# Another order of the same tasks on four engines in a software-pipelined attention loop

## Chip, cores and metric

One core of one Trainium2 chip runs the whole program. The metric is the device time of one execution in microseconds (us), the median of the runs shown.

## What is computed

A transformer layer with adaptive layer norms on 8 samples of 512 tokens with 256 features: a gated delta-rule attention (16 key heads, 32 value heads, head size 128) and a small mixture of experts. Nearly all the time goes to the attention. Cut to what matters:

```python
qkvz = hidden_states @ W_qkvz.T                  # q, k, v, z of all heads
mixed = silu(causal_conv4(q, k, v))              # 4 taps along the tokens
q, k = l2norm(q), l2norm(k)
g = cumsum(-exp(A_log) * softplus(a + dt_bias))  # inside a chunk
decay = where(tril, exp(g_i - g_j), 0)
A = -where(strict_tril, (k * beta) @ k.T * decay, 0)
T = solve_triangular(eye - A, eye)               # the inverse, chunk by chunk
value_, k_cumdecay = T @ v_beta, T @ (k_beta * exp(g))
for each chunk:                                  # scan with a state of 128 x 128
    v_new = v_i - kcd_i @ state
    out_i = (q_i * exp(g_i)) @ state + (q_i @ k_i.T * decay) @ v_new
    state = state * exp(g_last) + (k_i * exp(g_last - g_i)).T @ v_new
h = out * rsqrt(mean(out**2) + eps); h = norm_weight * h * silu(z)
y = h @ W_out.T
```

## The kernel before

Three stages run one after the other: `modulation_and_gates`, `attention` and `experts`. The change touches the attention stage alone.

**The loop.** The attention stage has 128 steps, one for each sample b and key head kh (8 x 16). A step handles one key head with its two value heads, in four chunks of 128 tokens, that is eight 128 x 128 units (U = 8). Its work is cut into tasks: 57 on PE, 63 on DVE, 41 on ACT, 16 on POOL. Each engine walks through its own list of tasks over and over: `PE_ORDER`, `ACT_ORDER`, `DVE_ORDER`, `POOL_ORDER` (lines 34 to 44). `M2@3` in the list means: part 2 of task M, for the step that lies 3 ahead of the number of this round. So one round of a list holds tasks of several steps, and a step goes through the engines over some four rounds. `loop` (in `attention`) writes the rounds before the first and after the last out in full and runs the middle ones two at a time in a hardware loop; how many are written out follows from `LEAD`, the largest number behind an @ in any list.

**What sets the order.** Within an engine, the list alone. Between engines, semaphores: each task waits for the tasks whose results it reads and for those that still read what it overwrites (`t.wait`), whatever the lists say. Nothing is planned at run time. SP, which issues the loads, has an order of its own (`FEEDS`), which no list touches.

**The tasks that matter here,** with the lines that the profile shows:

- P0 to P11 (PE, L658): the projections, two matmuls to a bank; C (ACT, L886) and T0 to T11 (DVE, L1018) do the convolution.
- KT, QT (PE, L668, L676): transposes of keys and queries; KN, QN on ACT square them, KN, QN on DVE (L1024, L1028) sum the squares. PW (POOL, L1199) takes the root of the sums.
- SM0 to SM3 (DVE, L1034, L1038, L1043, L1046): tiny operations of 128 x 8 elements that turn the roots into the factors `neg_c`. SM2 reads `inv` and `g_col`, SM3 `cc` and `inv`. SN0 (L1052) reads `neg_c` and `g_col` and makes `w_c`; SN1 (L1056) and SN2 (L1060) make scales of q. All these tensors lie in SBUF.
- KK0, KK1 (PE, L690): the products of keys with keys and queries into the two banks `p_out`. GL (POOL, L1194) and GE (ACT, L924, eight `Exp` and a load of the activation table) make `dec`, of which there is one buffer. GA0 to GA3 (DVE, L1072, eight operations) multiply the products with `neg_c` and `dec` into `ga`.
- SL (POOL, L1203), AB0 and AB1 (DVE, L1078), AO (ACT, L929), AR and AL (POOL, L1209, L1213) prepare the matrix A. L, M1 to M5 and Y1 to Y5 (PE), q1 to q5, y0 to y5, X1 to X5 (DVE, L1085, L1093, L1102), and XB1 to XB5 on ACT (L936) and on POOL (L1225) invert it level by level in one bank `p_lev`. s10, s11 (L1109), XD, Q6, p6, Z6, YC, XC join the halves.
- D0, D1 (PE, L764 to L766) compute the residual, F0, F1 (DVE, L1118) write it to `resid`, RL (POOL, L1217) splits it, G0, G1 (PE, L780), v0, v1 (ACT, L970), W0, W1 (PE, L796 to L798), IV0, IV1 (ACT, L966) finish the inverse.
- TR, VW, U, ST, KS, RR, SD, VX, O, OT, VK: the scan over the four chunks, on all engines. OQ, OS, OP, ON, HT: the norm of the output. OY0, OY1 (PE, L868): its projection, into the banks `p_out`; YA0, YA1 (DVE, L1170) add it up.

KT, VT, QT, KK, D, G, W, ON and OY share the two banks `p_out`. Each of them waits for the reader of what stood in the bank last (`wait_newest`, whose argument lists the other users of the bank, newest first). GL waits for GE of the step before, and GE for two things, in this order:

```python
elif name == "GE":
    t.wait(act, "g_low")
    t.wait(act, "ga_done", back=1)
    for u in range(U):
        last = act.activation(dec[:, u, :], low[:, u, :], ACT.Exp, bias=g_neg[p][:, u:u + 1])
    last.then_inc(s["decay"], 1)
```

Of the kernel before, what the change touches and what calls it, by code (L numbers as in the profile page):

```python
# [16 lines left out]
KT = D // P  # L17
# [13 lines left out]
Q_G, Q_BETA, Q_W, Q_EG, Q_GL = range(5)  # L31
NQ = 5
PAD = TAPS - 1
PE_ORDER = ("M2@3 ON1@1 O0@2 VT0@3 Y2@3 KS1@2 W1@2 M3@3 TR1@2 P0@4 Y3@3 U1@2 P1@4 M4@3 KS2@2 O1@2 P2@4 Y4@3 TR2@2 "
            "P3@4 M5@3 VT1@3 O2@2 U2@2 P4@4 KS3@2 Y5@3 P5@4 KT@4 QT@4 XD@3 Q6@3 TR3@2 P6@4 Z6@3 P7@4 D0@3 O3@2 XC@3 "
            "D1@3 KK0@4 KK1@4 P8@4 OY0@1 OY1@1 G0@3 L@4 P9@4 W0@3 M1@4 P10@4 TR0@3 Y1@4 G1@3 P11@4 U0@3 ON0@2")
ACT_ORDER = ("GE@2 OT3@0 C3@2 OQ3@0 XC@1 SV0@2 AO@2 v0@1 IV0@1 XB1@2 VX0@1 v1@1 SV1@2 XB2@2 OT0@1 Z0@2 Z1@2 XB3@2 "
             "IV1@1 VK0@2 VX1@1 C0@3 XB4@2 OT1@1 OQ0@1 VX2@1 C1@3 OQ1@1 XB5@2 OT2@1 VK1@2 OQ2@1 SK@3 SQ@3 C2@3 KN@3 "
             "QN@3 XD@2 VX3@1 KT@3 YC@2")
DVE_ORDER = ("T10@3 y0@3 T11@3 X1@3 q1@3 YA1@0 VW0@2 y1@3 X2@3 ST0@2 HT0@1 q2@3 HT1@1 y2@3 RR1@2 X3@3 q3@3 VW1@2 "  # L40
# [3 lines left out]
POOL_ORDER = ("SL@3 OP@1 XB1@3 ON@1 XB2@3 SD1@2 GL@4 XB3@3 QD@3 XB4@3 AR@3 SD2@2 AL@3 XB5@3 PW@4 RL@3")  # L44


def const_columns():
# [347 lines left out]
def attention(nc, io, scratch, const):  # L395


    with ExitStack() as ctx:
# [66 lines left out]
        SPARE = 3  # L465
        LEAD = max(int(name[-1]) for order in (PE_ORDER, ACT_ORDER, DVE_ORDER, POOL_ORDER) for name in order.split())

# [42 lines left out]
        def loop(eng, emit, order):  # L510
            for iteration in range(-LEAD, 0):
                run(eng, emit, order, fixed(iteration))
            rounds = (NIT - LEAD) // 2
            with eng.Fori(0, rounds) as m:
                for u in range(2):
                    run(eng, emit, order, lambda off: Step(m * 2 + (u + off), (u + off) % 2, m + (u + off) // 2))
            for iteration in range(rounds * 2, NIT):
                run(eng, emit, order, fixed(iteration))
# [126 lines left out]
        def _(pe):  # L645
# [225 lines left out]

            loop(pe, emit, PE_ORDER)

        @block.scalar
        def _(act):
# [120 lines left out]

            loop(act, emit, ACT_ORDER)

        @block.vector
        def _(dve):  # L1000
# [171 lines left out]

            loop(dve, emit, DVE_ORDER)

        @block.gpsimd
        def _(pool):
# [77 lines left out]

            loop(pool, emit, POOL_ORDER)

# [390 lines left out]
```

## Time and profile before

| | |
|---|---|
| median of 3 runs | 4839.93 us (4837.36 to 4840.07) |
| span of the profiled execution | 4831.3 us |
| PE, PE weight loads | busy 97%, 66% |
| DVE, ACT, POOL | busy 91%, 72%, 57% |
| DMA | 24.7% of 16 engines, 78 GB/s |
| mean granted TensorE clock | 0.987 |

The profile is of one execution. Busy time of an engine is the union of its instructions; overlapping ones count once. Line numbers (L658) are those of the kernel before. In a timeline, a record gives start, duration and what was executed, and in brackets the idle time of the engine ahead of it, if it is long, with the instruction that ended it. Neighbours of the same line are put together (x8), and their durations are then the stretch from the first start to the last end. The clock is a fraction of 2.4 GHz.

### The profile page before, as it was taken

How to read it: one execution, taken by the hardware profiler on the slowest of the kernel's cores; microseconds unless marked ns; L12 is line 12 of the kernel's file. 1: busy time of each engine (PE TensorE's matmuls, PEld its weight loads, DVE VectorE, ACT ScalarE, POOL GpSimd, SP SyncE). 2: the span in 40 equal slices, each digit the busy share in tenths (PEclk: the TensorE clock that was granted, in tenths of full speed). 3: DMA queues.
4: the chain of work that ended last, by engine and by line, in shares of the span. 5: the costliest groups of instructions: out<-in, count | busy, mean ns of one | idle time of the engine just before them, and what ended most of it. 6: DMA issues, size and time to landing. Idle time of an engine off the chain costs nothing. (4 is left out here: it accounts for less than half of the span.)

```text
span 4831.3 us, 132942 instructions
## 1 busy us (share of the span) xinstructions
PE 4671.0 (97%) x38533; PEld 3195.1 (66%) x38788; DVE 4411.5 (91%) x9152; ACT 3467.6 (72%) x8336; POOL 2743.0 (57%) x2329
## 2 busy tenths in 40 slices
PE   5899999999999999999999999999999999999978
PEld 3566666666666666666666666666666666666643
DVE  4899999999999999999999999999999999999953
ACT  3677777777777777777777777777777777777732
POOL 2456665656565665656566665656566665656520
PEclk7999999999999999999999999999999999999988
DMA  4222222222222222222222222222222222222122
GB/s 156 65 75 79 68 86 70 88 66 87 67 79 79 68 86 71 88 66 87 67 80 79 68 86 66 92 66 84 70 78 80 66 87 66 92 66 84 55 79 83
DMA packets 185165, 377.26 MB, mean 78 GB/s; under 512 B 86400, under 2 KB 95744, under 8 KB 184960
## 3 DMA queue, kind: packets, MB, share of 16 engines
q1 hardware_dynamic: 185088, 376.46, 24.7%
q14 instruction: 57, 0.47, 0.0%
q8 instruction: 20, 0.33, 0.0%
HBM read 360.13 MB, written 16.25 MB: 78 GB/s over the span
## 5 line engine op out<-in xcount | busy, mean ns | idle before, releaser
L658 PE MATMUL p_proj<-hid,w_in 128*128 128x512 f32 x3072 | 1626.7, 612 | 30.0 <-POOL ident_h L1185 28.9
L1018 DVE SCALAR_TENSOR_TENSOR conv<-p_proj,taps,conv 128x509 f32<-128x509 f32 (+2 forms) x1536 | 1134.8, 739 | 48.2 <-ACT conv L886 34.9
L1199 POOL TENSOR_TENSOR root<-sums,half_pow 128x8 f32<-128x8 f32 x128 | 210.8, 1647 | 862.9 <-DVE sums L1028 843.9
L1225 POOL TENSOR_SCALAR_AFFINE_SELECT x_bd<-x_t 128x512 bf16<-128x512 bf16 x640 | 422.6, 660 | 213.5 <-DVE x_t L1102 211.2
L658 PEld LDWEIGHTS p_proj<-hid,w_in 128*128 128x128 f32 x3072 | 497.3, 192 | 55.1 <-POOL ident_h L1185 29.1
L1093 DVE TENSOR_TENSOR y_h<-p_lev,y_h 128x512 bf16<-128x512 f32 x640 | 440.2, 688 | 74.4 <-PE p_lev L725 74.4
L868 PE MATMUL p_out<-h_t,w_out 128*128 128x512 f32 x1024 | 476.5, 608 | 2.2 <-DVE h_t L1164 1.1
L936 ACT ACTIVATE x_bd<-x_t 64x512 bf16<-64x512 bf16 x640 | 397.7, 621 | 96.3 <-DVE x_t L1102 96.2
L1102 DVE STREAM_TRANSPOSE x_t<-y_h 128x512 bf16<-128x512 bf16 x640 | 450.3, 704 | 4.5
L1072 DVE SCALAR_TENSOR_TENSOR ga<-p_out,neg_c,dec 128x256 f32<-128x256 f32 x1024 | 412.9, 477 | 35.4 <-ACT dec L924 34.8
L886 ACT ACTIVATE conv<-p_proj,taps 128x512 f32<-128x512 f32 x512 | 351.7, 687 | 121.9 <-PE p_proj L658 119.3
L1085 DVE TENSOR_TENSOR q_h<-p_lev,consts 128x512 bf16<-128x512 f32 x640 | 429.6, 671 | 3.8 <-PE p_lev L718 3.8
L979 ACT ACTIVATE vx<-p_b 128x256 f32<-128x256 f32 x512 | 197.9, 386 | 285.8 <-PE p_b L816 161.4
L1217 POOL TENSOR_TENSOR r_lo<-resid 128x1024 bf16<-128x1024 f32 x128 | 242.3, 1893 | 247.9 <-DVE resid L1118 247.9
L838 PE MATMUL p_b<-vx,ga 128*128 128x128 f32 x2048 | 375.1, 275 | 0.0
L868 PEld LDWEIGHTS p_out<-h_t,w_out 128*128 128x128 f32 x1024 | 184.6, 190 | 285.0 <-DVE ga L1072 147.9
L725 PEld LDWEIGHTS p_lev<-q_h,x_bd 128*128 128x128 bf16 x5120 | 216.5, 97 | 213.5 <-issue 101.5
L985 ACT ACTIVATE o_tok<-p_b 128x256 f32<-128x256 f32 x512 | 194.1, 379 | 199.5 <-PE p_b L838 196.4
L718 PEld LDWEIGHTS p_lev<-y_h,a_bd 128*128 128x128 bf16 x5120 | 222.7, 98 | 152.1 <-issue 84.2
L1232 POOL TENSOR_TENSOR q_dec<-kq,e_row 128x512 f32<-128x512 f32 x256 | 320.0, 1271 | 0.0
L924 ACT ACTIVATE dec<-low,g_neg 128x128 f32<-128x128 f32 x1024 | 313.3, 388 | 1.6
L1244 POOL TENSOR_TENSOR o_sc<-o_sc,neg_half 128x8 f32<-128x8 f32 x128 | 211.4, 1651 | 168.9 <-DVE o_sc L1159 168.9
(213 smaller groups left out, 12562.4 us busy)
## 6 DMA issues: line engine op xcount, KB each, us to landing
w_in<-in_w_in SPq DMA_DIRECT2D x128, 768.0 KB, 6.3
g_row<-rows_scratch SPq DMA_DIRECT2D x128, 512.0 KB, 3.2
hid<-h_scratch SPq DMA_DIRECT2D x128, 512.0 KB, 7.4
e_row<-exp_rows_scratch SPq DMA_DIRECT2D x128, 512.0 KB, 5.3
w_out<-in_w_out SPq DMA_DIRECT2D x128, 256.5 KB, 2.7
x<-in_x SPq DMA_DIRECT2D x8, 512.0 KB, 10.6
h_scratch<-x SPq DMA_DIRECT2D x8, 512.0 KB, 2.6
y_scratch<-y_acc SPq DMA_DIRECT2D x8, 512.0 KB, 6.1
```

The costliest lines, as they stand in the source:

```text
L658: last = pe.matmul(p_proj[tile % 2][:], w_in[p][:, kt, tile * P:(tile + 1) * P], hid[p][:, kt, :], start=(kt == 0), stop=(kt == KT - 1))
L838: last = pe.matmul(p_b[:, at], ga[p][:, n * HD + h, 1, :], vx[:, h, :], start=(n == 0), stop=True)
L868: last = pe.matmul(p_out[n][:], w_out[p][:, h * D + n * P:h * D + (n + 1) * P], h_t[:, :, h, :], start=(h == 0), stop=(h == HD - 1))
L886: act.activation(conv[:, n, :], p_proj[n % 2][:], ACT.Copy, scale=taps[p][:, n, PAD:PAD + 1])\
L936: act.activation(x_bd[0:HB, :, 0:HB], x_t[0:HB], ACT.Copy).then_inc(s["xbd"], 1)
L1018: dve.scalar_tensor_tensor(conv[:, tile, late:], p_proj[tile % 2][:, 0:S - late], taps[p][:, tile, j:j + 1], conv[:, tile, late:], ALU.mul ...
L1072: last = dve.scalar_tensor_tensor(ga[p][:, u], kk, neg_c[p][:, n, h:h + 1], each(dec[:, u, :], 2), ALU.mult, ALU.mult)
L1085: dve.tensor_tensor(q_h[:], levels(), each(const["mask"][:, n * HB:(n + 1) * HB], U), ALU.mult)\
L1093: dve.tensor_tensor(y_h[:], levels(), y_h[:], ALU.add).then_inc(s["y_done"], 1)
L1102: dve.transpose(x_t[:].rearrange("p u f -> p (u f)"), y_h[:].rearrange("p u f -> p (u f)"))\
L1225: pool.affine_select(x_bd[:, :, HB:P], x_t[:], [[0, U], [0, HB]], ALU.is_ge, zero, base=-HB, channel_multiplier=1).then_inc(s["xbd_low"], 1)
L1232: last = pool.tensor_tensor(q_dec[p][:, :, h, :], kq[p][:, :, 1, :], e_row[p][:].rearrange("p (c h) i -> p c h i", h=HD)[:, :, h, :], ALU. ...
```

## The change

The four lists are replaced by others. They hold the same tasks; in each list some stand in another place, and some are taken from another step. The order in which the tasks use the two banks `p_out` is the same as before in either bank, and the lists in `wait_newest` stay as they are. The largest number behind an @ becomes 5 (GL@5), so that one more round is written out ahead of the loop and the hardware loop ends earlier.

```diff
-PE_ORDER = ("M2@3 ON1@1 O0@2 VT0@3 Y2@3 KS1@2 W1@2 M3@3 TR1@2 P0@4 Y3@3 U1@2 P1@4 M4@3 KS2@2 O1@2 P2@4 Y4@3 TR2@2 "
-            "P3@4 M5@3 VT1@3 O2@2 U2@2 P4@4 KS3@2 Y5@3 P5@4 KT@4 QT@4 XD@3 Q6@3 TR3@2 P6@4 Z6@3 P7@4 D0@3 O3@2 XC@3 "
-            "D1@3 KK0@4 KK1@4 P8@4 OY0@1 OY1@1 G0@3 L@4 P9@4 W0@3 M1@4 P10@4 TR0@3 Y1@4 G1@3 P11@4 U0@3 ON0@2")
-ACT_ORDER = ("GE@2 OT3@0 C3@2 OQ3@0 XC@1 SV0@2 AO@2 v0@1 IV0@1 XB1@2 VX0@1 v1@1 SV1@2 XB2@2 OT0@1 Z0@2 Z1@2 XB3@2 "
-             "IV1@1 VK0@2 VX1@1 C0@3 XB4@2 OT1@1 OQ0@1 VX2@1 C1@3 OQ1@1 XB5@2 OT2@1 VK1@2 OQ2@1 SK@3 SQ@3 C2@3 KN@3 "
-             "QN@3 XD@2 VX3@1 KT@3 YC@2")
-DVE_ORDER = ("T10@3 y0@3 T11@3 X1@3 q1@3 YA1@0 VW0@2 y1@3 X2@3 ST0@2 HT0@1 q2@3 HT1@1 y2@3 RR1@2 X3@3 q3@3 VW1@2 "
-             "y3@3 ST1@2 X4@3 q4@3 T0@4 RR2@2 T1@4 y4@3 VW2@2 X5@3 T2@4 q5@3 T3@4 ST2@2 T4@4 T5@4 y5@3 SN1@3 s11@3 "
-             "s10@3 RR3@2 T6@4 p6@3 KN@4 QN@4 T7@4 T8@4 SN2@3 F0@3 SM0@4 SM1@4 SM2@4 SM3@4 F1@3 SN0@3 GA0@4 GA1@4 "
-             "GA2@4 GA3@4 T9@4 YA0@1 OS0@2 AB0@4 AB1@4 OS1@2")
-POOL_ORDER = ("SL@3 OP@1 XB1@3 ON@1 XB2@3 SD1@2 GL@4 XB3@3 QD@3 XB4@3 AR@3 SD2@2 AL@3 XB5@3 PW@4 RL@3")
+PE_ORDER = ("ON0@1 O0@2 ON1@1 KS1@2 Y2@3 VT0@3 W1@2 M3@3 TR1@2 P0@4 Y3@3 U1@2 P1@4 M4@3 KS2@2 O1@2 Y4@3 P2@4 TR2@2 P3@4 U2@2 "
+            "VT1@3 O2@2 KS3@2 M5@3 P4@4 KT@4 Y5@3 P5@4 QT@4 Q6@3 XD@3 P6@4 TR3@2 Z6@3 P7@4 D0@3 D1@3 O3@2 KK0@4 XC@3 KK1@4 "
+            "P8@4 OY0@1 OY1@1 G0@3 L@4 P9@4 W0@3 M1@4 P10@4 TR0@3 G1@3 Y1@4 P11@4 U0@3 M2@4")
+ACT_ORDER = ("XD@1 QN@2 YC@1 OQ0@0 VX3@0 OQ1@0 SV0@2 OT3@0 OQ2@0 XC@1 OQ3@0 C3@2 GE@3 v0@1 IV0@1 XB1@2 v1@1 VX0@1 SV1@2 XB2@2 "
+             "Z0@2 OT0@1 XB3@2 Z1@2 AO@2 VX1@1 VK0@2 C0@3 XB4@2 IV1@1 OT1@1 VX2@1 C1@3 VK1@2 XB5@2 SK@3 OT2@1 SQ@3 KN@3 KT@3 "
+             "C2@3")
+DVE_ORDER = ("YA1@0 q1@3 VW0@2 y1@3 X2@3 ST0@2 q2@3 HT0@1 HT1@1 y2@3 RR1@2 X3@3 q3@3 VW1@2 SN1@3 y3@3 ST1@2 X4@3 q4@3 T0@4 "
+             "RR2@2 T1@4 y4@3 VW2@2 X5@3 T2@4 ST2@2 T3@4 T4@4 q5@3 T5@4 SN2@3 y5@3 s11@3 s10@3 RR3@2 p6@3 T6@4 T7@4 KN@4 QN@4 "
+             "T8@4 F0@3 F1@3 SM0@4 SM1@4 SM2@4 SN0@3 SM3@4 GA0@4 GA1@4 GA2@4 GA3@4 T9@4 YA0@1 OS0@2 AB0@4 AB1@4 T10@4 OS1@2 "
+             "y0@4 T11@4 X1@4")
+POOL_ORDER = ("OP@1 XB1@3 ON@1 XB2@3 XB3@3 SD1@2 XB4@3 QD@3 SD2@2 XB5@3 AR@3 AL@3 PW@4 RL@3 GL@5 SL@4")
```

Read round the circle, and with the steps counted from the same task, the lists differ in these places:

- PE: M2 ahead of ON0; O0 between ON0 and ON1; KS1 ahead of Y2 and VT0 behind it; Y4 ahead of P2; U2 ahead of VT1 and O2; KS3 ahead of M5 and P4; KT ahead of Y5; Q6 ahead of XD; P6 ahead of TR3; D1 right behind D0, XC between KK0 and KK1; G1 ahead of Y1.
- DVE: ST2 ahead of T3; q5 between T4 and T5; SN2 ahead of y5, SN1 behind VW1; p6 ahead of T6, T7 ahead of the two sums; F1 right behind F0; SN0 between SM2 and SM3; OS1 behind T10; YA1 ahead of q1; q2 ahead of HT0.
- ACT: GE from right behind YC to right behind C3, for the next step; OQ0 to OQ2 and OT2 later, by up to half a round; QN behind XD; SV0 ahead of OT3; v1 ahead of VX0; OT0 between Z0 and Z1's new place behind XB3; AO from ahead of v0 to behind Z1; IV1, VK1 and KT in other places by one to four tasks.
- POOL: GL from behind SD1 to right behind RL, ahead of SL; SD1 behind XB3; QD behind XB4, AR and AL behind XB5.

## Rows read from the trace of the kernel before

**Rows 1.** The page, one line of its 40 slices: granted TensorE clock in tenths.
```profile
PEclk7999999999999999999999999999999999999988
```
**Rows 2.** One line's instructions: count, ns min/median/max, first and last start in us.
```profile
L1072 DVE SCALAR_TENSOR_TENSOR ga<-p_out,neg_c,dec x1024: 473/476/485, 134.2 to 4592.7; 128x256 f32<-128x256 f32 x171
```
**Rows 3.** Timeline of DVE, 2410.9 to 2418.8 us: start, duration, engine, line, operation.
```profile
2410.89 0.68 DVE L1028 TENSOR_REDUCE sums<-squares 128x4 f32<-128x512 f32 x1
...
2413.05 0.16 DVE L1060 TENSOR_SCALAR q_s<-inv 128x4 f32<-128x4 f32 x1
2413.12 0.69 DVE L1118 TENSOR_TENSOR resid<-p_out,consts 128x512 f32<-128x512 f32 x1
2413.72 0.17 DVE L1034 TENSOR_SCALAR neg_n<-root 128x8 f32<-128x8 f32 x1
...
2414.36 0.17 DVE L1046 SCALAR_TENSOR_TENSOR neg_c<-cc,inv 128x8 f32<-128x8 f32 x1
2414.47 0.69 DVE L1118 TENSOR_TENSOR resid<-p_out,consts 128x512 f32<-128x512 f32 x1
...
2415.57 3.23 DVE L1072 SCALAR_TENSOR_TENSOR ga<-p_out,neg_c,dec 128x256 f32<-128x256 f32 x8 [0.33 <-ACT dec L924]
```
**Rows 4.** Timeline of POOL, from 2402 to 2429 us, same columns.
```profile
2402.55 1.89 POOL L1213 TENSOR_TENSOR a_lo<-a_rest 128x1024 bf16<-128x1024 f32 x1
2404.40 0.66 POOL L1225 TENSOR_SCALAR_AFFINE_SELECT x_bd<-x_t 128x512 bf16<-128x512 bf16 x1
...
2411.80 1.65 POOL L1199 TENSOR_TENSOR root<-sums,half_pow 128x8 f32<-128x8 f32 x1 [6.74 <-DVE sums L1028]
2415.24 1.89 POOL L1217 TENSOR_TENSOR r_lo<-resid 128x1024 bf16<-128x1024 f32 x1 [1.79 <-DVE resid L1118]
...
2428.41 2.35 POOL L1194 TENSOR_TENSOR low<-g_row,consts 128x1024 f32<-128x1024 f32 x1
```
**Rows 5.** Timelines of DVE and POOL, around 207 us and around 4624 us.
```profile
207.40 0.71 DVE L1156 TENSOR_TENSOR o_sc<-o_ss,q_s 128x8 f32<-128x8 f32 x1
207.00 1.10 POOL L1203 TENSOR_SCALAR_AFFINE_SELECT ga<-ga 128x1024 f32<-128x1024 f32 x1 [1.81 <-DVE ga L1072]
...
4624.25 0.26 DVE L1156 TENSOR_TENSOR o_sc<-o_ss,q_s 128x8 f32<-128x8 f32 x1
4622.59 1.89 POOL L1217 TENSOR_TENSOR r_lo<-resid 128x1024 bf16<-128x1024 f32 x1 [8.39 <-DVE resid L1118]
```
**Rows 6.** Timeline of PE, 2407 to 2421 us.
```profile
2407.44 0.60 PE L668 MATMUL p_out<-consts,kq 128*128 128x128 f32 x4
...
2411.67 0.22 PE L764 MATMUL p_out<-y_dn,ga 128*128 128x128 bf16 x1
...
2416.24 1.02 PE L658 MATMUL p_proj<-hid,w_in 128*128 128x512 f32 x2
2417.28 3.70 PE L868 MATMUL p_out<-h_t,w_out 128*128 128x512 f32 x8
```
**Rows 7.** Timeline of ACT, 2411 to 2422 us, and one row of 4738.87 us.
```profile
2411.62 1.28 ACT L924 ACT_TABLE_LOAD   x1
2412.92 2.45 ACT L924 ACTIVATE dec<-low,g_neg 128x128 f32<-128x128 f32 x8
...
2421.24 0.60 ACT L970 ACTIVATE g_t<-p_out 128x512 bf16<-128x512 f32 x1 [0.52 <-PE p_out L780]
...
4738.87 1.28 ACT L1466 ACT_TABLE_LOAD   x1 [12.08 <-PE p_h L1397]
```
**Rows 8.** Timeline of PE, the filling of the loop: 172 us and 209 us.
```profile
172.25 0.61 PE L713 MATMUL p_lev<-eye_h,a_bd 128*128 128x64 bf16 x8 [3.27 <-DVE a_bd L1078]
...
209.05 0.61 PE L713 MATMUL p_lev<-eye_h,a_bd 128*128 128x64 bf16 x8 [3.12 <-DVE a_bd L1078]
```
**Rows 9.** Busy us (and instructions) by window; then granted clock, DMA share, GB/s.
```profile
171.39:178.22 6.83, 5.75 (x32) 3.74 (x34) 4.09 (x7) 2.14 (x4) 0.66 (x1) 0.50 0.29 90
...
208.94:212.35 3.41, 3.08 (x16) 1.81 (x18) 2.75 (x6) 0.29 (x1) 2.29 (x3) 0.50 0.38 147
```

## Prediction

> **Names.** Tasks are named without their @; times behind "F0 at 0" are in us from F0's start. F is the pair of `resid` adds on DVE, SM0 to SM3 and SN0 the tiny 128x8 operations behind the key norms, GA the eight gated products, PW, RL, GL, SL the POOL tasks of L1199, L1217, L1194, L1203, GE the eight exponentials of L924, OY the output projection, L the first matmul group of a solve, KK the products of keys.
>
> **What bounds the kernel now.** First the page: its slices show PE at 9 tenths in all the middle, with TensorE's granted clock at 1.00 there, the 2.4 GHz level, and lower only at both ends [rows 1]. Then the period. The eight GA of a step are 128 groups between 134.2 and 4592.7 us; the last start is the eighth of its group, some 2.75 us behind the first, so a step takes (4592.7 - 2.75 - 134.2) / 127 = 35.08 us [rows 2]. The loop is 127 periods of the 4831; everything else here is a sum within one period. Then the timelines of the engines. PE has hardly a hole, and DVE neither: in the stretch from the key sums to GA, only GA waits, 0.33 us, for GE [rows 3]. So no engine has a large reserve. What the order can lose is much larger than what it can win: a new wait on DVE that PE cannot pass lengthens every period by itself.
>
> **The order around the key norms.** Before, from F0 on DVE: F0 at 2413.12, SM0 at 2413.72 (0.60 later), SM3 at 1.24 with SM1 and SM2 in between, F1 at 1.35, then SN0, GA at 2.45 [rows 3]. On POOL, PW runs from 2411.80 to 2413.45, and then nothing until RL at 2415.24, which is 0.08 behind the end of F1 (2414.47 + 0.69) [rows 4]. So SM2, SM3 and SN0, which read two tensors of SBUF each, all fall into a time in which POOL is idle.
>
> The new lists put F1 right behind F0, ahead of SM0, and SN0 between SM2 and SM3; POOL gets GL right behind RL. RL waits for F1 alone, since PW ends earlier. With F0 at 0: F1 ends at 0.60 + 0.69 = 1.29, RL starts at 1.37 and ends at 3.26. SM0 needs PW: the second key sum started at 2410.89, SM0 at 2413.72, 2.83 later and nearly all of it PW [rows 3, 4]. Between that sum and F0 stands now only T8, at 0.71 + 0.66, so SM0 can't start before 2.83 - 1.37 = 1.46, which is inside RL. SM3 stood 0.64 behind SM0 [rows 3], SM2 0.2 ahead of SM3, so SM2 comes to about 1.90.
>
> **What a two-input operation does under POOL.** The trace has it twice, where OS0, the same 128x8 shape as SM2 and SM3 (SM3 0.17 us [rows 3]), runs while POOL reads SBUF. In the filling of the loop it starts at 207.40 under SL (207.00 to 208.10) and takes 0.71 us; in the draining it starts at 4624.25 under RL (4622.59 to 4624.48) and takes 0.26. Both end within 0.03 us of the end of POOL's operation [rows 5]. So SM2 is held until 3.27. SM3 needs SM2's result and starts 0.03 later, at 3.30. But POOL starts a queued task before the last one's record ends: a_lo at 2402.55 takes 1.89, and the next started at 2404.40 [rows 4]. GL, whose waits are long met, starts at 1.37 + 1.85 = 3.22, ahead of SM3, and takes 2.35 [rows 4]: to 5.57. SM3 ends there, and GA0 starts at 5.65; 5.9 if SN0 is the one held and SM3 follows it. Before it was 2.45. **This is +3.2 us on DVE** (3.45 at the upper end; 0.8 at the lower, if GL lets SM3 pass). The 0.33 us that GA waited for GE is won back inside this number.
>
> The Trainium skill, SBUF — State Buffer, section Who interferes with whom, says the same of two SBUF inputs, and adds that `tensor_scalar` and copies in a 2-port mode are held too. The row of SN2, a `tensor_scalar`, speaks against the addition for this shape: it took 0.16 us at 2413.05, under PW [rows 3, 4]. SN2 moves to just ahead of y5, where the last POOL task is AL; by that rule y5 would be held for up to 0.8 us more per period, some 100 us in all. I leave it out of the sum.
>
> **Who waits for GA.** OY0 overwrites the bank that GA0 and GA1 read, and PE is in order. PE's part from D0 to the end of P8 is the same work as before: it started at 2411.67, 1.45 ahead of F0, and ended at 2416.24 + 1.02, so at F0 + 4.1 [rows 6]. OY0 can start when GA1 ends; GA0 and GA1 are half of 3.23 [rows 3]: 5.65 + 1.65 + 0.05 = 7.35. Before, it started at 2417.28 with P8 just in front [rows 6]. So PE stands still for 3.2 us in each period.
>
> **The rest of the period.** From GA to the next F0 it was 35.08 - 2.45 = 32.6 us. SL still waits for GA (it started right behind it, and GL has ended by then), so AB and L keep their distance. GE's new place is behind C3 and ahead of v0: it can start when GA ends, 5.65 + 3.23 = 8.9, its table load (1.28) having run under GA, and with 2.45 it ends at 11.35 [rows 7]; v0 needs G0, behind the 3.70 of OY, about 7.35 + 3.7 + 0.2 = 11.25 [rows 6]. It costs nothing there, as long as GA is late. The second load goes from SV0 to SV1, between VX0 and XB2; XB2 then ends some 0.1 us ahead of the time at which PE comes to Y2. The transposes KT, 0.60 us by their record [rows 6], of which the next group overlaps a part, now stand ahead of Y5, so y5 is 0.4 later. On the other side q2 ahead of HT0, KS1 ahead of Y2, YA1 ahead of q1 and Y4 ahead of P2 take waits of a tenth or two away, each below what a row names as idle; my estimate from the starts is 0.8 in all, between 0.4 and 1.2. AO, OQ0 to OQ2, AR, AL, SD1 and M5 move inside slack of more than a microsecond. Net -0.4, between -0.8 and 0. The period is 5.65 + 32.2 = 37.85 us, at full clock.
>
> **The clock.** Twice in the filling PE stood still for about as long as it now will in each period: 3.27 us before 172.25, 3.12 before 209.05 [rows 8]. After both the granted clock was 0.50, the 1.2 GHz level, for 6.83 and 3.41 us, with PE busy 5.75 and 3.08 us of it [rows 9]. Work at half clock loses half of its time: 2.9 and 1.5 us, 2.2 on average. OY, G0, L and P9 stand there, and after GA's delay PE is the last to arrive. I count three of four gaps: +1.7, bounds 0 and 2.9. Period 39.5.
>
> **Sum.** (39.5 - 35.1) x 126 = 4.4 x 126 = 555, on the profiled span of 4831: 5386. The median of the runs, 4839.9, lies 8.6 us above that span: **5395 us**. Filling and draining have the same tasks (one more unrolled step at each end, which only holds GL); I count nothing. No DMA gets on the path: g_row is fetched a period before GL.
>
> **Rivals.** (1) The lock as above, but the clock stays at 2.4 GHz after most gaps: 37.85, + 2.8 x 126 = 350, so 5190 us. For it: two gaps are few, they lie in the filling, where other waits surround them, and the loop's gap has unbroken work on both sides. Against it: the gaps are as long as these [rows 8, 9]. (2) DVE gets its turn between RL and GL, or SBUF reads don't collide in steady state. Then GL becomes the bound in another way. GE needs GL's end, and its table load stands behind that wait: at 4738.87 a load came only after 12.08 us of idle [rows 7], behind the first wait of its instruction. From F0: 1.29 to F1's end, then 0.08 + 1.85 + 2.35 + 0.1 + 1.28 + 2.45 = 8.1 to v0. From v0 to the next F0 it was 2413.12 + 35.08 - 2421.24 = 27.0 [rows 3, 7], less the 0.4 from above: 36.0, or 35.6 if v0's slack of some 0.4 before W0 is used up. That gives + 0.55 to 0.9 x 126: 4910 to 4955. The skill, ScalarE: Activation LUTs, section What ACT_TABLE_LOAD costs, adds a drain of about 1.38 us to a load; in the rows the exponentials start 0.02 us behind the load's end [rows 7], so I give it nothing. (3) **Faster**: no collision, and the load runs ahead of GL's wait. Then GE costs nothing, the short waits are won, F0 to GA takes 2.3 in place of 2.45, and PE has nearly no wait left: 35.08 - 0.4 - 0.15 = 34.5 us, -0.58 x 126 = -73, so 4767. It needs SM3 to end by 2.3 behind F0, and v0 to start within 0.3 us of G0's end; it decides at SM2's duration, 0.17 or over a microsecond. Against it stand both rows of OS0. (4) No change: (2) with errors of sum that cancel.
>
> **Chances.** Forecast 0.57, (1) 0.25, (2) 0.11, (3) 0.04, (4) 0.03. The range of the first two is 5130 (rival 1 with the rest at -0.8) to 5620 (every gap at half clock, GA at 5.9), 8 in 10 with their tails. About 0.2%, 10 us, is what can be told from no change: faster 0.04, same 0.03, slower 0.93.
>
> **What would show it.** Right: SM2 at 1.4 us and SM3 or SN0 at over 2 in place of 0.17; GA idle before it for a few tenths at most, since the time is in the durations; PE idle about 3.2 us before L868, released by GA of L1072; clock at 0.5 in many slices; GE's idle before L924 gone. Wrong: SM2 at 0.17 (the lock falls), PE gaps without a lower clock (the 1.7 falls), or idle before L970 put down to L924 (rival 2).

## The result and the profile after

The changed kernel takes **5456.02 us** (median of 4 runs, 5450.64 to 5458.91) against 4838.65 (4836.20 to 4840.07): the ratio is 1.1275, with a 95% interval of 1.1259 to 1.1291. The forecast was 5395 in a range of 5130 to 5620. The profiled execution has a span of 5455.8 us, 624.5 more than before, with the same work.

The page of the changed kernel: the granted clock, and three rows of its groups (busy us, mean ns of one, then idle time before them and what ended it).

```profile
PEclk7899999999999999999999999999999999999999
...
L868 PE MATMUL p_out<-h_t,w_out 128*128 128x512 f32 x1024 | 644.9, 789 | 429.6 <-DVE ga L1072 428.5
...
L924 ACT ACTIVATE dec<-low,g_neg 128x128 f32<-128x128 f32 x1024 | 313.0, 387 | 273.0 <-DVE ga L1072 245.9
...
L1072 DVE SCALAR_TENSOR_TENSOR ga<-p_out,neg_c,dec 128x256 f32<-128x256 f32 x1024 | 412.9, 476 | 14.4 <-DVE neg_c L1046 11.7
```

PE now stands still for 429.6 us ahead of OY, 3.4 in each step, and GA ends that. One matmul of OY takes 789 ns on average; it took 608. The lines of DVE (count, ns min/median/max, first and last start) say why GA is late:

```profile
L1072 DVE SCALAR_TENSOR_TENSOR ga<-p_out,neg_c,dec x1024: 473/476/485, 138.1 to 5219.2; 128x256 f32<-128x256 f32 x171
...
L1043 DVE TENSOR_TENSOR cc<-inv,g_col x128: 168/1512/1601, 137.7 to 5214.5; 128x8 f32<-128x8 f32 x128
...
L1046 DVE SCALAR_TENSOR_TENSOR neg_c<-cc,inv x128: 166/2273/2277, 137.9 to 5216.1; 128x8 f32<-128x8 f32 x128
...
L1052 DVE TENSOR_TENSOR w_c<-neg_c,g_col x128: 152/154/156, 172.5 to 5250.2; 128x8 f32<-128x8 f32 x128
...
L1060 DVE TENSOR_SCALAR q_s<-inv x128: 306/1142/1466, 162.6 to 5240.9; 128x4 f32<-128x4 f32 x128
```

The period is (5219.2 - 2.75 - 138.1) / 127 = 39.99 us, where it was 35.08 [rows 2]. SM2 and SM3 take 1.51 and 2.27 us in place of 0.17 [rows 3]; and SN2 takes 1.14 in place of 0.16. The timelines of DVE and then POOL (start, duration) show beside what they run:

```profile
2406.32 1.14 DVE L1060 TENSOR_SCALAR q_s<-inv 128x4 f32<-128x4 f32 x1
...
2413.26 1.28 DVE L1118 TENSOR_TENSOR resid<-p_out,consts 128x512 f32<-128x512 f32 x2
2414.58 0.17 DVE L1034 TENSOR_SCALAR neg_n<-root 128x8 f32<-128x8 f32 x1
2414.79 0.20 DVE L1038 RECIPROCAL inv<-neg_n 128x8 f32<-128x8 f32 x1
2415.03 1.51 DVE L1043 TENSOR_TENSOR cc<-inv,g_col 128x8 f32<-128x8 f32 x1
2416.46 0.15 DVE L1052 TENSOR_TENSOR w_c<-neg_c,g_col 128x8 f32<-128x8 f32 x1
2416.57 2.27 DVE L1046 SCALAR_TENSOR_TENSOR neg_c<-cc,inv 128x8 f32<-128x8 f32 x1
2418.88 3.23 DVE L1072 SCALAR_TENSOR_TENSOR ga<-p_out,neg_c,dec 128x256 f32<-128x256 f32 x8
```
```profile
2405.54 1.90 POOL L1213 TENSOR_TENSOR a_lo<-a_rest 128x1024 bf16<-128x1024 f32 x1
2412.91 1.64 POOL L1199 TENSOR_TENSOR root<-sums,half_pow 128x8 f32<-128x8 f32 x1 [5.47 <-DVE sums L1028]
2414.62 1.89 POOL L1217 TENSOR_TENSOR r_lo<-resid 128x1024 bf16<-128x1024 f32 x1
2416.47 2.35 POOL L1194 TENSOR_TENSOR low<-g_row,consts 128x1024 f32<-128x1024 f32 x1
```

SM2 ends with RL (2416.54 and 2416.51), SM3 with GL (2418.84 and 2418.82), SN2 with AL (2407.46 and 2407.44). Below, such an operation is said to be held by the POOL task beside it. GA starts 5.62 us behind F0. PE and ACT behind it:

```profile
2416.21 1.02 PE L658 MATMUL p_proj<-hid,w_in 128*128 128x512 f32 x2
2420.59 3.70 PE L868 MATMUL p_out<-h_t,w_out 128*128 128x512 f32 x8 [3.36 <-DVE ga L1072]
```
```profile
2418.92 1.28 ACT L924 ACT_TABLE_LOAD   x1 [1.71 <-POOL low L1194]
2422.14 2.45 ACT L924 ACTIVATE dec<-low,g_neg 128x128 f32<-128x128 f32 x8 [1.94 <-DVE ga L1072]
2424.56 0.60 ACT L970 ACTIVATE g_t<-p_out 128x512 bf16<-128x512 f32 x1
```

In this step OY ran at full clock, 3.70 us. In the next it took 5.40, and the view of a stretch in it shows the 1.2 GHz level, right behind a gap of 3.52 us (the columns are those of [rows 9]):

```profile
2459.42 5.40 PE L868 MATMUL p_out<-h_t,w_out 128*128 128x512 f32 x8 [3.52 <-DVE ga L1072]
```
```profile
2459.93:2463.34 3.41, 3.41 (x5) 1.35 (x4) 2.07 (x5) 2.37 (x8) 1.10 (x1) 0.50 0.00 0
```

From 400 to 5000 us, 115 periods, the trace has 82 such stretches, 65 of 3.41 us and 17 of 6.83. Of 110 middle steps the 31 whose OY ran at full clock take 38.75 us, all together 40.00.

### The profile page after: what moved, and what is told of

Same layout as the page of the kernel before. It is cut to its first block and busy times, and to the rows that moved or that the text cites. A ratio compares the mean times of both kernels' runs of the same rounds, so it can differ in the third digit from the quotient of the medians.

```text
span 5455.8 us, 133429 instructions
## 1 busy us (share of the span) xinstructions
PE 4839.6 (89%) x38788; PEld 3291.8 (60%) x38788; DVE 4949.2 (91%) x9152; ACT 3519.1 (65%) x8334; POOL 2759.7 (51%) x2329
## 5 line engine op out<-in xcount | busy, mean ns | idle before, releaser
L658 PE MATMUL p_proj<-hid,w_in 128*128 128x512 f32 x3072 | 1657.7, 622 | 32.3 <-POOL ident_h L1185 28.7
L868 PE MATMUL p_out<-h_t,w_out 128*128 128x512 f32 x1024 | 644.9, 789 | 429.6 <-DVE ga L1072 428.5
L868 PEld LDWEIGHTS p_out<-h_t,w_out 128*128 128x128 f32 x1024 | 243.7, 249 | 822.3 <-DVE ga L1072 554.4
L924 ACT ACTIVATE dec<-low,g_neg 128x128 f32<-128x128 f32 x1024 | 313.0, 387 | 273.0 <-DVE ga L1072 245.9
L1203 POOL TENSOR_SCALAR_AFFINE_SELECT ga<-ga 128x1024 f32<-128x1024 f32 x128 | 140.6, 1098 | 453.1 <-DVE ga L1072 453.1
L970 ACT ACTIVATE g_t<-p_out 128x512 bf16<-128x512 f32 x256 | 152.8, 597 | 267.0 <-PE p_out L780 266.2
L994 ACT ACTIVATE o_junk<-o_tok 128x128 f32<-128x128 f32 x1024 | 303.3, 299 | 3.2
```

Source lines behind the costliest of these rows:

```text
L658: last = pe.matmul(p_proj[tile % 2][:], w_in[p][:, kt, tile * P:(tile + 1) * P], hid[p][:, kt, :], start=(kt == 0), stop=(kt == KT - 1))
L868: last = pe.matmul(p_out[n][:], w_out[p][:, h * D + n * P:h * D + (n + 1) * P], h_t[:, :, h, :], start=(h == 0), stop=(h == HD - 1))
```

## The experiments

Periods are worked out from the first and last GA, as above. "F0 to GA" and "gap", PE's idle time ahead of OY, are means over 110 middle steps of the trace. "Stretches" counts those at a granted clock of 0.50 in the loop, per 100 periods. The ratio is to the kernel before on the same chip.

| kernel | us | ratio (95%) | period | F0 to GA | gap | stretches |
|---|---|---|---|---|---|---|
| before | 4838.65 | 1 | 35.08 | 2.47 | none | 0 |
| changed | 5456.02 | 1.1275 (1.1259 to 1.1291) | 39.99 | 5.70 | 3.4 | 71 |
| e2_one_input | 4987.52 | 1.0312 (1.0294 to 1.0329) | 36.25 | 2.44 | 0.2 | 0 |
| e4_gl_back | 5090.21 | 1.0522 (1.0504 to 1.0539) | 37.06 | 3.70 | 1.4 | 0 |
| e3_f1_back | 5181.41 | 1.0711 (1.0693 to 1.0729) | 37.78 | 2.85 | none | 0 |
| e1_fill_pe | 5310.20 | 1.0982 (1.0964 to 1.1001) | 38.78 | 5.70 | 0.9 | 0 |
| e6_sn2_back | 5507.54 | 1.1392 (1.1373 to 1.1411) | 40.35 | 5.70 | 3.4 | 100 |
| e10_sn2_fill | 5220.39 | 1.0799 (1.0782 to 1.0816) | 38.08 | 5.71 | 0.9 | 0 |
| e7_before_f1 | 5146.63 | 1.0651 (1.0633 to 1.0669) | 37.54 | 4.44 | 2.1 | 30 |
| e11_before_f1_d1 | 4996.68 | 1.0335 (1.0320 to 1.0351) | 36.39 | 3.76 | 1.6 | 0 |
| e5_both_back | 4995.36 | 1.0338 (1.0320 to 1.0355) | 36.33 | 2.86 | none | 0 |
| e8_three_back | 4896.44 | 1.0133 (1.0116 to 1.0150) | 35.56 | 2.79 | none | 0 |
| e9_t7_back | 4818.66 | 0.9969 (0.9957 to 0.9981) | 34.95 | 2.25 | none | 0 |

**The inputs alone.** The order stays, the operations read one SBUF tensor each:

```diff
-  dve.tensor_scalar(neg_n[p][:], root[:], 1e-6, -1.0, ALU.add, ALU.mult)
+  dve.tensor_scalar(neg_n[p][:], root[:], 1e-6, -16.0, ALU.add, ALU.mult)
-  dve.tensor_tensor(cc[:], inv_k, beta, ALU.mult)
+  dve.reciprocal(cc[:], inv_k)
-  dve.scalar_tensor_tensor(neg_c[p][:], cc[:], -1.0, inv_k, ALU.mult, ALU.mult)
+  dve.reciprocal(neg_c[p][:], cc[:])
-  dve.tensor_tensor(w_c[p][:], neg_c[p][:], w, ALU.mult)
+  dve.reciprocal(w_c[p][:], over(neg_n[p][:, 0, :], [P, NC, HD]))
```

> The changed kernel with all lists and waits as they are, but SM2, SM3 and SN0 are reciprocals, which read one SBUF tensor in place of two (and the factor in SM0 is -16 in place of -1, to keep numbers small). The factors beta and w are left out, so the result is another one; number, order, shapes and waits of the instructions stay. THEORY (the two SBUF inputs are held by POOL): each takes about 0.2 us, GA starts at F0 + 2.6 in place of 5.7. Then GL sets the end: RL and GL end at F0 + 5.6, the table load at 6.95, GE at 9.4, v0 there, and from v0 to the next F0 27.35 us as in the changed kernel at full clock: 36.75 us per period, 4839 + (36.75 - 35.07) x 126 = 5050 us (4990 to 5110), clock at 1.00 in nearly all steps. RIVAL A (the long durations are a wait for RL's or GL's result or of DVE's pipeline, whatever the inputs): 5456, the three operations at 1.46 and 2.27. RIVAL B (no bound behind the hold): GE is no limit, 35.8 us per period, 4930.

```profile
L1043 DVE RECIPROCAL cc<-inv x128: 202/203/206, 137.4 to 4741.7; 128x8 f32<-128x8 f32 x128
...
L1046 DVE RECIPROCAL neg_c<-cc x128: 202/203/204, 137.6 to 4741.9; 128x8 f32<-128x8 f32 x128
```

Both take 0.20 us in all steps, although they run wholly beside RL, so it is neither the order nor a wait. The factors beta and w are left out here, and the operation changed together with what it reads. That it isn't the kind of operation, GA shows: it is a `SCALAR_TENSOR_TENSOR` as SM3 is, but takes one large input from a PSUM bank, and its eight run in 3.23 us partly beside RL [rows 3, 4], none longer than 0.485 us [rows 2]. In e3_f1_back they stand beside RL (2446.37 to 2448.27) and GL, and over 370 of them ran wholly under each, in at most 0.48 us:

```profile
2446.28 3.22 DVE L1072 SCALAR_TENSOR_TENSOR ga<-p_out,neg_c,dec 128x256 f32<-128x256 f32 x8
```

GL starts where it did, but SM3 is done by then. GA came 3.26 us earlier, and 3.74 us of period went, 1.24 of it the clock's part (below, with PE's gap filled). What is left is the rival with no collision (2), here in its timeline of ACT:

```profile
2352.45 1.28 ACT L924 ACT_TABLE_LOAD   x1 [1.73 <-POOL low L1194]
2353.74 2.45 ACT L924 ACTIVATE dec<-low,g_neg 128x128 f32<-128x128 f32 x8
2356.10 0.58 ACT L970 ACTIVATE g_t<-p_out 128x512 bf16<-128x512 f32 x1
```

GL, load, exponentials and v0 stand in a row. v0 starts at F0 + 9.31 (expected 9.4); from there to the next F0 it is 26.95 us, not 27.35, which together makes the run 62 us faster than expected, a little below its range.

**GL alone back:**

```diff
-  SD1@2 XB4@3 QD@3 SD2@2 XB5@3 AR@3 AL@3 PW@4 RL@3 GL@5 SL@4
+  SD1@2 GL@5 XB4@3 QD@3 SD2@2 XB5@3 AR@3 AL@3 PW@4 RL@3 SL@4
```

> The changed kernel with GL alone back behind SD1 on POOL; F1 stays ahead of SM0. THEORY: RL still holds SM2 for 1.4 to 1.5 us, but nothing follows RL, so SN0 and SM3 take 0.15 to 0.17 us. GA at F0 + 3.6 in place of 5.7, PE's gap ahead of OY 1.2 us and the clock at 1.00 behind it; GE starts when GA ends, at 6.85, v0 at 9.3, 9.3 + 27.35 = 36.65 us per period, 4839 + 1.58 x 126 = 5040 us (4990 to 5110). RIVAL (GL is not what holds SM3): SM3 stays at 2.27 us and the time near 5456.

```profile
L1043 DVE TENSOR_TENSOR cc<-inv,g_col x128: 166/1503/1599, 139.0 to 4844.5; 128x8 f32<-128x8 f32 x128
...
L1046 DVE SCALAR_TENSOR_TENSOR neg_c<-cc,inv x128: 166/167/169, 139.2 to 4846.1; 128x8 f32<-128x8 f32 x128
```

RL alone holds SM2, and SM3's hold goes with GL. GA is at F0 + 3.70 (3.6 expected). The time is 50 us above the expected one, because v0 comes at 9.41 and from there to the next F0 it takes 27.63 us.

**F1 and SN0 alone back:**

```diff
-  T8@4 F0@3 F1@3 SM0@4 SM1@4 SM2@4 SN0@3 SM3@4 GA0@4
+  T8@4 F0@3 SM0@4 SM1@4 SM2@4 SM3@4 F1@3 SN0@3 GA0@4
```

> The changed kernel with F1 and SN0 back where they were: F0, SM0 to SM3, F1, SN0, GA. All else stays, GL right behind RL too. THEORY: nothing two-input falls under POOL, SM2 and SM3 at 0.17 us, GA at F0 + 2.9 in place of 5.7. But RL now starts later, behind F1 at F0 + 2.8, so GL ends at 7.0, the table load at 8.4, GE at 10.85, v0 there: 10.85 + 27.35 = 38.2 us per period, 4839 + 3.1 x 126 = 5230 us (5150 to 5330, the upper part if the wait of W0 for v0 brings a low clock). So most of the loss stays although the hold is gone: a new wait in its place, ACT's v0 waiting for POOL's GL by way of the table load. RIVAL (the hold was all of it): GA at 2.9 gives a period of 35.9 at full clock, 4945 us.

Timelines of POOL and ACT of that run:

```profile
2446.37 1.90 POOL L1217 TENSOR_TENSOR r_lo<-resid 128x1024 bf16<-128x1024 f32 x1 [1.56 <-DVE resid L1118]
2448.22 2.36 POOL L1194 TENSOR_TENSOR low<-g_row,consts 128x1024 f32<-128x1024 f32 x1
```
```profile
2450.68 1.28 ACT L924 ACT_TABLE_LOAD   x1 [3.20 <-POOL low L1194]
2451.97 2.45 ACT L924 ACTIVATE dec<-low,g_neg 128x128 f32<-128x128 f32 x8
2454.32 0.57 ACT L970 ACTIVATE g_t<-p_out 128x512 bf16<-128x512 f32 x1
```

The hold ahead of GA is gone (SM2 and SM3 at 0.17 us), OY follows P8 without a gap, and still 2.7 us per period stay. The row that tells it is the load, which waits 3.20 us for GL. Under the hold the same chain was hidden: in the changed kernel the load ran under GA, and v0 started within 0.1 us of the end of G0. The later SL brings a new hold: OS0 (L1156, two SBUF inputs) takes 0.67 to 0.84 us to SL's end in every middle step, where it took 0.16. From v0 to the next F0 it is 26.95 us as in e2_one_input, where OS0 isn't held, so it shows no cost here.

**PE's gap filled:** three more products like P8's first, into the bank that P8 then overwrites.

```diff
+  for i in range(3 if n == 8 else 0):
+      pe.matmul(p_proj[0][:], w_in[p][:, 0, tile * P:(tile + 1) * P], hid[p][:, 0, :], start=True, stop=True)
```

> The changed kernel with the first product of P8 computed three more times into the same bank, so that PE has some 2.6 us of its own work inside the 3.4 us in which it waited for GA. Nothing that is used changes. THEORY (lock plus clock): in the changed kernel's trace 79 of 110 middle steps run OY wholly or partly at the 1.2 GHz level and take 40.49 us, the 31 others 38.75. With the gap cut to about 0.8 us the clock stays at 1.00, OY takes 3.70 us in every step, SM2 and SM3 stay at 1.46 and 2.27 us, the period is 38.75 and the time 5456 - (40.00 - 38.75) x 126 = 5298 us (5270 to 5330). RIVAL (the clock falls for another reason than the gap, or its fall costs nothing because DVE sets the period): 5456 or a little more, OY at 3.08 + 2.73 us on average as before.

```profile
2428.05 3.70 PE L869 MATMUL p_out<-h_t,w_out 128*128 128x512 f32 x8 [0.80 <-DVE ga L1073]
```
```profile
1000.00:2000.00 1000.00, 967.75 (x7871) 660.61 (x7869) 970.05 (x1803) 692.61 (x1655) 552.89 (x467) 1.00 0.22 70
```

PE has more to do, and the kernel is 146 us faster. The hold is the same (2.28 us on SM3), the clock is at 1.00, and the period is that of the full-clock steps. So the clock's part is 40.00 - 38.76 = 1.24 us per period.

**SN2 alone back:**

```diff
-  T5@4 SN2@3 y5@3 ... T8@4 F0@3
+  T5@4 y5@3 ... T8@4 SN2@3 F0@3
```

> The changed kernel with SN2 alone back behind T8, ahead of F0. In the changed kernel SN2 (a tensor_scalar of 128x4) starts under AL and takes 1.14 us in every step, ending with AL; before it took 0.16 under PW. THEORY (POOL holds the tensor_scalar too, and y5 to F0 is on the path): SN2 takes 0.16 us, the period loses 0.8 to 1.0 us of the 40.0, the clock's part stays: 5456 - 0.9 x 126 = 5345 us (5320 to 5390). RIVAL A (SN2 is late for another reason and takes as long in its new place, or SM0 comes later by as much): 5456. RIVAL B (DVE has slack there, the hold costs nothing): 0.16 us, but 5440 to 5460.

SN2 took 0.16 us as expected, and the kernel became 51 us slower: my expectation had the wrong sign. A window of it, in which OY took 6.58 us:

```profile
2438.95:2445.78 6.83, 5.84 (x7) 2.52 (x8) 5.11 (x13) 3.05 (x9) 1.10 (x1) 0.50 0.00 0
```

There are 114 stretches in 114 periods, 76 of them of 6.83 us, behind gaps no longer than in the changed kernel. To take the clock out, the next run has both edits:

> The changed kernel with SN2 back behind T8 and with the three extra products in PE's gap. SN2's move alone made the kernel slower (5508), although SN2 took 0.16 us in place of 1.14; OY was slowed in all of 110 middle steps in place of 79. THEORY (the move is worth 0.7 us per period, as with GL and F1 taken back, but more gaps end at the 1.2 GHz level): with the gap filled the clock stays at 1.00 and the period is 38.75 - 0.7 = 38.05, so 4834 + 2.98 x 126 = 5210 us (5180 to 5240), some 90 us below the filled kernel without the move (5310). RIVAL (the move itself costs time under the hold): at or above 5310.

38.08 against 38.78 us: without the clock, SN2's hold costs 0.70 us per period. With it, the gain was more than eaten up. Why nearly the same gap lowers the clock in 71 of 100 steps in one kernel and in all of the other stays open. In e6_sn2_back 94 of 113 neighbouring stretches start 40.96 us apart, and its steps take 39.5 to 41.1 us, so it looks as if it mattered where in time a gap falls; no run varied that alone.

**F1 alone, in the kernel before:**

```diff
-  F0@3 SM0@4 SM1@4 SM2@4 SM3@4 F1@3 SN0@3 GA0@4
+  F0@3 F1@3 SM0@4 SM1@4 SM2@4 SM3@4 SN0@3 GA0@4
```

> The kernel before with one move alone: F1 right behind F0, ahead of SM0. GL stays behind SD1, all other lists as before. THEORY: F1 ends at F0 + 1.29, RL starts at 1.37 and holds SM2 to 3.25, SM3 and SN0 follow at 0.17 each, GA at F0 + 3.6 in place of 2.47: + 1.1 us per period, PE's gap about 1.0 us with the clock at 1.00, 4837 + 1.1 x 126 = 4975 us (4940 to 5000). RIVAL (the hold comes only with the rest of the new order, or SM2 ends ahead of RL): SM2 at 0.17, within 10 us of 4837.

```profile
2420.82 0.69 DVE L1118 TENSOR_TENSOR resid<-p_out,consts 128x512 f32<-128x512 f32 x1 [0.59 <-PE p_out L766]
...
2421.86 1.65 DVE L1043 TENSOR_TENSOR cc<-inv,g_col 128x8 f32<-128x8 f32 x1
```
```profile
2421.59 1.90 POOL L1217 TENSOR_TENSOR r_lo<-resid 128x1024 bf16<-128x1024 f32 x1 [1.72 <-DVE resid L1118]
```

The hold was as expected; 172 us were missed by a wait. In the old PE order D1 stands behind O3 and XC, and F1, now early, waits for it. The gap became 2.1 us, and OY was slowed in 32 of 110 steps. With D1 right behind D0 as well:

```diff
-  D0@3 O3@2 XC@3 D1@3 KK0@4
+  D0@3 D1@3 O3@2 XC@3 KK0@4
```

> The kernel before with F1 right behind F0, as in the run that gave 5147, and with D1 on PE right behind D0, as in the changed kernel. In that run F1 waited 0.59 us for D1, RL started at F0 + 2.04 and GA came at F0 + 4.44, with PE's gap 2.09 us and OY at a lower clock in 32 of 110 steps. THEORY: without the wait RL starts at F0 + 1.36 and all of it comes 0.67 earlier: GA at F0 + 3.77, gap 1.4 us, the clock at 1.00 in all steps as behind the 1.45 us gap of the run with GL taken back, 36.4 us per period, 4834 + 1.33 x 126 = 5000 us (4970 to 5030). RIVAL (the wait for D1 was covered by the one for PW or by the hold): 5147.

GA at F0 + 3.76, 36.39 us, clock at 1.00: on the number. In the changed kernel, too, D1 stands behind D0; the two moves belong together.

**What is left of the loss.** Both moves back, with the edits of e3_f1_back and e4_gl_back together; then SN2 too, with that of e6_sn2_back; then T7 as well:

```diff
-  T6@4 T7@4 KN@4 QN@4 T8@4
+  T6@4 KN@4 QN@4 T7@4 T8@4
```

> The changed kernel with both moves taken back: F1 and SN0 behind SM3, GL behind SD1. Everything else of the change stays. THEORY: no two-input operation under POOL around the key norms and no GL ahead of GE. GA at F0 + 2.85, as measured with F1 alone taken back; the table load runs under GA, GE from 6.1 to 8.55, v0 at 8.6, then 26.95 us to the next F0, as in the two runs in which PE had no gap: 35.5 us per period, 4837 + 0.45 x 126 = 4893 us (4860 to 4940). So these two moves hold all but a percent of the loss. RIVAL (the rest of the new order costs much by itself): above 4940. RIVAL (the rest of the new order is a gain): below 4837.

> The changed kernel with three moves taken back: F1 and SN0, GL, and SN2 (behind T8). THEORY: as with the first two taken back (35.5 us per period), less the 0.5 to 1.0 us by which SN2's hold delays y5 and what follows it: 34.5 to 35.0 us, so 4770 to 4837, most likely 4820, and faster than the kernel before if the shorter waits of the new PE order are worth anything. RIVAL (PE or DVE work sets the period and SN2's hold was covered): the same as with two taken back.

> The kernel with three moves taken back, and with T7 too back behind the two key sums. With T7 ahead of them the sum of the queries stands only 1.4 us ahead of F0, PW ends 1.26 us behind F0, and DVE waits for it ahead of SM0; before, SM0 came 0.60 behind F0. THEORY: that wait is the rest of the loss against the kernel before (35.55 us per period against 35.07): SM0 at F0 + 0.60, GA at F0 + 2.2, the period 35.0 to 35.2, 4834 + 0.03 x 126 = 4838 us (4820 to 4855), no difference from the kernel before. RIVAL A (GE's new place or the new PE order holds the rest): 4880 to 4900 as without this move. RIVAL B (the new PE order is a gain once nothing hides it): below 4820.

The first came out 102 us above the expectation and the second 76, both outside their ranges. In both I had mis-stated v0 to the next F0. For the first I carried over 26.95 us from e2_one_input and e3_f1_back, in which v0 stood 1.2 and 2.3 us behind the end of G0; for the second I took SN2's hold off that figure once more. With v0 within 0.1 us of G0's end it is 27.60 with the hold and 26.91 without it, again 0.7. So behind a late v0 nearly all of SN2's hold was covered; this is argued from these figures, and no run tests it alone. What then still stood against the kernel before is a wait for PW, in the timelines of DVE with three moves back (first) and with T7 back (second):

```profile
2302.10 0.17 DVE L1034 TENSOR_SCALAR neg_n<-root 128x8 f32<-128x8 f32 x1 [0.57 <-POOL root L1199]
```
```profile
2264.25 0.16 DVE L1034 TENSOR_SCALAR neg_n<-root 128x8 f32<-128x8 f32 x1
```

Moving T7 is worth 0.61 us per period. The last kernel is **faster than both**: 4818.66 us, 0.31% below the kernel before (0.19 to 0.43). The expectation was 4838 (4820 to 4855), no difference. The kernel keeps the new PE and ACT lists, with GE in its new place; there the table load runs ahead of GA's end and GA no longer waits for GE. F0 to GA is 2.25 us in place of 2.47, and from GA to the next F0 nothing is won (32.68 us against 32.59). So the gain stands where GA waited for GE, not in the new PE order that rival B named; no run moved GE alone.

## Why the prediction was right, step by step

Over 110 middle steps a period grew by 4.93 us, from 35.07 to 40.00: 3.22 from F0 to GA, 0.70 for SN2, -0.23 for the rest of the order, and 1.24 for the clock. The forecast was 3.2, 0, -0.4 and 1.7. The hold, PE's gap and the clock were in their right places. That the sum came within 61 us is in part luck: the 0.70 that was left out is set off by 0.46 too much for the clock.

- **The hold.** SM0 at F0 + 1.32 (predicted 1.46), RL at 1.36 (1.37), GL at 3.21 (3.22), GA at 5.70 (5.65). Of the two ways in which SN0 and SM3 could follow RL the first holds: SN0 passes between RL and GL in 0.15 us in every step, SM3 is held to GL's end. That it is the second SBUF input, e2_one_input shows; that it is these two POOL tasks, e3_f1_back and e4_gl_back.
- **PE's gap.** 3.44 us on average for 3.2, released by GA, as said.
- **SN2, the step that failed.** I took the 0.16 us of one row, under PW [rows 3, 4], for what a `tensor_scalar` costs under POOL, and left 0.8 us per period out of the sum. Under AL, SN2 was held in every middle step, and it cost 0.70 us. The Trainium skill (SBUF — State Buffer, Who interferes with whom) names `tensor_scalar` in a 2-port mode among what can contend with GpSimd; the runs with AL agree, 1.14 us against 0.16, though no view shows in which mode SN2 ran. Under PW it took 0.16 us in every middle step of all kernels that have it there. So the one row was true, but of PW only: which POOL task stands beside it decides. PW works on 128x8 elements and AL on 128x1024; whether it is that, no run separates.
- **The rest of the order.** With the SN2 part taken out it is 32.36 us from GA to the next F0 against 32.59, so -0.23, inside the bounds of -0.8 to 0.
- **The clock.** Three of four gaps was near (82 in 115 periods), but I took both lengths of stretch as equally likely. 65 of 82 were the short one, and one stretch cost 1.24 / 0.71 = 1.7 us, not 2.2.
- **Rival (1)**, without the clock: its price was right, e1_fill_pe gives it at 5310, with SN2's hold in it. **Rival (2)** exists behind the hold: e2_one_input is this case. It cost 36.25 us where I had 35.6 to 36.0; SN2's hold is in it. **Rival (3)**, the faster one, needs more than that the collision goes: e9_t7_back, without any hold, comes to 34.95, not 34.5.
- **The range.** Its ends don't follow exactly from the terms that it names. They give 5139 us (37.45 us per period) and 5586 us (41.0 us per period) in place of 5130 and 5620; the measured time lies inside either way.
- **Signs.** "The clock at 0.5 in many slices" was ill put: a slice is 136 us long and averages, so the page shows 9 tenths. "GE's idle before L924 gone" was wrong as written: ACT now stands 273.0 us ahead of it, its table loaded, and waits for GA. What went is GA's wait for GE, 0.33 us per step before [rows 3] and none now.

## What to carry to other kernels

Before moving a small VectorE operation, look at what GpSimd runs at its new time, and for how many elements; an operation of 0.17 us with two SBUF inputs took 1.51 and 2.27 us here, to the end of the GpSimd task beside it, and the task queued right behind took the next turn as well. Such a delay shows as a duration, not as a wait, so a list of waits doesn't tell of it. And when one cause is taken back, ask which chain it had covered: here more than half of the loss (343 of 617 us) stayed, in another place, when F1's way back had removed the hold.

## What the hardware showed that I had not expected

- A `reciprocal` with one SBUF input wasn't held at all: SM1 takes 0.20 us wholly under RL, and the three of e2_one_input took 0.15 to 0.20 under RL.
- A two-input operation that stands ready when one POOL task ends can get in ahead of the next queued one (SN0, 0.15 us at 2416.46, where GL's record starts at 2416.47), but the one behind it, SM3, was held. SN1 (two inputs, 0.14 us at 2396.52) passes in the same way, between an XB that ends at 2396.54 and a POOL task that starts at 2396.51.
- Gaps in PE of 0.9, 1.4 and 1.6 us were followed by no stretch at the 1.2 GHz level, gaps of 2.1 us by 34 in 115 periods, and gaps of 3.4 us by 82 in 115 or by one in each, depending on the kernel. Less wait on DVE can thus make a kernel slower, and more work on PE can make it faster by 146 us.
